# GpSimd's layer-3 bias adds and FFN weight halves moved into layers 1 and 2 of a graph network kernel

## What is computed

```python
xn = _layernorm(x)
# gnn: three layers, widths 256 -> 1024 -> 512 -> 256, each
#   gcn_conv (h = x @ W, summed over edges with coef dinv[src]*dinv[dst]) + b, relu, layer_norm * gamma + beta
x = x + gnn(xn, edges) + mix(xn)
# ffn on xn2 = _layernorm(x): a router picks 1561 of the 3125 nodes...
sel = take_along_axis(xn2, sel_idx)
y = (gelu(sel @ w1 + b1) @ w2 + b2) * w_sel
x = x + (xn2 + scatter(y))
```

## Time and profile before

| what | value |
|---|---|
| median of 3 runs | 1459.4 us (1458.06 to 1460.7) |
| profiled execution, its own time | 1460.05 us |
| its span in the profile | 1458.2 us |
| its mean granted TensorE clock | 0.959 of full speed |
| busy: PE / DVE / ACT / POOL | 1283.3 / 821.0 / 524.8 / 530.6 us |

### The profile page before, as it was taken

One profiled execution on the slowest core, in us unless ns is written; L12 is line 12 of the kernel. 1 busy time (PEld: TensorE's weight loads), 2 busy tenths in 40 slices (PEclk: granted clock), 3 DMA queues, 4 the chain that ended last, 5 costly groups with the idle time before them and its releaser, 6 DMA issues.

```text
span 1458.2 us, 20220 instructions
## 1 busy us (share of the span) xinstructions
PE 1283.3 (88%) x7100; PEld 866.5 (59%) x7100; DVE 821.0 (56%) x1478; ACT 524.8 (36%) x984; POOL 530.6 (36%) x542
## 2 busy tenths in 40 slices
PE   1996776897679999999999999999999999778985
PEld 1763453654446666666665666666666555457775
DVE  6566677868745545454553222222222998878675
ACT  3323626458532222222221232222221212248952
POOL 1003777777767777776000000000004840223000
PEclk9988888998879999999999999999999999989998
DMA  9860000000323232222210422212222444110002
GB/s 270 285 228 1 1 1 1 1 1 1 90 69 82 52 76 50 75 61 65 72 43 24 121 65 65 64 46 62 64 64 66 131 126 129 44 44 1 1 1 88
DMA packets 46192, 99.52 MB, mean 68 GB/s; under 512 B 19079, under 2 KB 31252, under 8 KB 46002
## 3 DMA queue, kind: packets, MB, share of 16 engines
q1 hardware_dynamic: 32814, 98.55, 23.8%
q0 software_dynamic: 13312, 0.13, 0.7%
HBM read 75.79 MB, written 22.85 MB: 68 GB/s over the span
## 4 chain that ended last, share of the span: by engine, by line
PE 66%; DVE 20%; ACT 5%; issue 5%; DMA 1%; POOL 1%; SPq 0%; DVEq 0%; ACTq 0%; POOLq 0%
PE psum L1705 63%; DVE scr L1216 4%; DVE scr L948 3%; PE psum L2066 1%; DVE scr L1174 1%; ACT scr L1367 1%; POOL acc L571 1%; DVE scr L1167 1%; DVE big L1151 1%; DVE scr L1178 1%; DMA rows<-in_x 1%; DVE scr L1164 1%; DVE scr L1161 1%; DVE acc L1233 1%; PE psum L2044 1%
## 5 line engine op out<-in xcount | busy, mean ns | idle before, releaser
L550 POOL DMA_INDIRECT counts<-big,eidx x416 | 422.7, 1016 | 252.7 <-issue 130.9
L1705 PE MATMUL psum<-rows,scr 125*125 125x512 f16 x1250 | 278.3, 381 | 11.5 <-DVE scr L1164 9.3
L1705 PE MATMUL psum<-big,scr 125*125 125x512 f16 x1250 | 278.5, 379 | 1.0 <-DVE big L1068 1.0
L1705 PEld LDWEIGHTS psum<-rows,scr 125*125 125x125 f16 x1250 | 170.4, 137 | 113.3 <-DVE scr L1164 10.0
L1705 PEld LDWEIGHTS psum<-big,scr 125*125 125x125 f16 x1250 | 169.9, 137 | 95.2 <-DVE big L1068 1.5
L566 POOL MEMSET big<- 128x4 f16 x1 | 0.1, 115 | 422.1 <-PE psum L1705 422.1
L1705 PE MATMUL psum<-wb,scr 128*125 128x512 f16 x600 | 137.5, 379 | 1.4 <-DVE scr L1051 1.4
L1032 DVE TENSOR_SCALAR scr<-psum,col 125x256 f32<-125x256 f32 x25 | 12.1, 485 | 172.1 <-PE psum L1705 172.1
L1705 PEld LDWEIGHTS psum<-wb,scr 128*125 128x125 f16 x600 | 81.1, 136 | 45.8 <-DVE scr L1051 1.9
L1705 PE MATMUL psum<-big,wm 128*128 128x313 f32 x312 | 95.0, 455 | 12.3 <-ACT big L1420 7.2
L1705 PE MATMUL psum<-wb,big 128*125 128x256 f16 x600 | 75.7, 280 | 23.8 <-DVE big L1227 21.1
(11 more groups left out here) (367 smaller groups left out, 1909.1 us busy)
## 6 DMA issues: line engine op xcount, KB each, us to landing
scr<-counts SPq DMA_DIRECT2D x75, 683.6 KB
counts<-wb SPq DMA_DIRECT2D x25, 683.6 KB
counts<-big,eidx POOLq DMA_INDIRECT x416
scr<-counts SPq DMA_DIRECT2D x75, 79.3 KB
scr<-in_x SPq DMA_DIRECT2D x25, 125.0 KB
rows<-in_x SPq DMA_DIRECT2D x5, 560.0 KB
out<-acc SPq DMA_DIRECT2D x5, 560.0 KB
wb<-in_w SPq DMA_DIRECT2D x1, 2048.0 KB, 10.6
```

What stands on the lines that cost most here:

```text
L550: pool.indirect_dma_start(cells, bass.IndirectOffsetOnAxis(ap=eidx[:, r * EQ + g:r * EQ + g + 1], axis=0), evalue[:, at_c:at_c + 1], None, ...
L1705: return pe.matmul(o, l, r, start=start, stop=stop)
```

## The change

GpSimd's program is put in another order: the 25 adds of `be3` and the eight weight pieces now stand ahead of the two clears of pad columns. The adds wait for `fx_done` of all 25 tiles, which DVE reaches in the last tile of layer 1, and for rows loaded long before. The pieces wait for `fscale_done`. To give these scales earlier, the PE sums, ACT's root and DVE's seven small instructions move from the front of layer 3 to a point after tile 8 of layer 2. For that, tiles 5 to 8 of layer 2 are written out on PE, DVE and ACT, and their loop runs 4 passes (from 1 to 4) in place of 5. No computation is added or left out.

```diff
 # GpSimd
-        pool.wait_ge(sem("rows1_ready"), T)
-        pool.memset(free(nT16[1], P * G, ...), 0.0).then_inc(sem("npad_done"), 1)
-        pool.wait_ge(sem("lo2_done"), T)
-        pool.wait_ge(sem("agg_done"), 2 * T)
-        pool.memset(free(nT16[0], P * G, ...), 0.0).then_inc(sem("npad_done"), 1)
-
         pool.wait_ge(sem("rowa_loaded"), 16 * 5)
         pool.wait_ge(sem("fx_done"), T)
         for t in range(T):
             pool.tensor_tensor(accv[:, t, :], accv[:, t, :], be3r, ALU.add).then_inc(sem("be3_added"), 1)
         pool.wait_ge(milestone("fscale_done"), AFTER["fscale_done"])
...
+        pool.wait_ge(sem("rows1_ready"), T)
+        pool.memset(free(nT16[1], P * G, ...), 0.0).then_inc(sem("npad_done"), 1)
+        pool.wait_ge(sem("lo2_done"), T)
+        pool.wait_ge(sem("agg_done"), 2 * T)
+        pool.memset(free(nT16[0], P * G, ...), 0.0).then_inc(sem("npad_done"), 1)
 # VectorE, layer 2
-        for t in range(HEAD):
+        for t in range(HEAD + RING):
             step2(t, t % 2, first=t == 0)
-        with dve.Fori(0, LOOPS) as i:
+        dve.wait_ge(milestone("fnorm_done"), AFTER["fnorm_done"])
+        (the seven instructions that end in fscale_done, from ahead of layer 3)
+        with dve.Fori(1, LOOPS) as i:
 # ScalarE, layer 2
         ffn_norms()
-        with act.Fori(0, LOOPS) as i:
+        for t in range(HEAD, HEAD + RING):
+            step2(t, t % 2)
+        ffn_norms_rooted()
+        with act.Fori(1, LOOPS) as i:
...
-        ffn_norms_rooted()
         root3_(0)
 # TensorE, layer 2
-        with pe.Fori(0, LOOPS) as i:
+        for t in range(HEAD, HEAD + RING):
+            step2(t, t, None)
+        pe.wait_ge(sem("fsquares_done"), 1)
+        (the 10 matmuls that end in fsum_done, from ahead of layer 3)
+        with pe.Fori(1, LOOPS) as i:
```

More of the change, by code:

```diff
@@ L561, in _ @@
                            pattern=[[-1, 128]], channel_multiplier=1).then_inc(sem("tri"), 1)
-        pool.wait_ge(sem("rows1_ready"), T)
-        pool.memset(free(nT16[1], P * G, [[CW, 4], [1, 1]]), 0.0).then_inc(sem("npad_done"), 1)
-        pool.wait_ge(sem("lo2_done"), T)
-        pool.wait_ge(sem("agg_done"), 2 * T)
-        pool.memset(free(nT16[0], P * G, [[CW, 4], [1, 1]]), 0.0).then_inc(sem("npad_done"), 1)
         pool.wait_ge(sem("rowa_loaded"), 16 * 5)
@@ L583, in _ @@
             pool.wait_ge(sem("fpiece_done"), c + 1)
+        pool.wait_ge(sem("rows1_ready"), T)
+        pool.memset(free(nT16[1], P * G, [[CW, 4], [1, 1]]), 0.0).then_inc(sem("npad_done"), 1)
+        pool.wait_ge(sem("lo2_done"), T)
+        pool.wait_ge(sem("agg_done"), 2 * T)
+        pool.memset(free(nT16[0], P * G, [[CW, 4], [1, 1]]), 0.0).then_inc(sem("npad_done"), 1)
         def stage_rows(c):
@@ L1124, in step2 @@
                 normalise(t, pre[b][:, 0:D2], D2, "relu2_done", "xhat2_done")
-        for t in range(HEAD):
+        for t in range(HEAD + RING):
             step2(t, t % 2, first=t == 0)
-        with dve.Fori(0, LOOPS) as i:
+        dve.wait_ge(milestone("fnorm_done"), AFTER["fnorm_done"])
+        done.did(dve.tensor_scalar(f_back, fnorm[:, 0:2], 1e-20, 1.0 / F16_TOP, ALU.max, ALU.mult))
+        done.did(dve.tensor_scalar(g_back, fnorm[:, 0:1], float(D) ** 0.5, fnorm[:, 2:3], ALU.mult, ALU.add))
+        done.settle()
+        done.did(dve.tensor_scalar(g_back, g_back, 1e-20, 1.0 / F16_TOP, ALU.max, ALU.mult))
+        done.did(dve.tensor_scalar(hid_back, f_back[:, 0:1], 1.0 / NORMED, None, ALU.mult))
+        done.settle()
+        done.did(dve.reciprocal(g_scale, g_back))
+        done.did(dve.tensor_tensor(out_back, g_back, f_back[:, 1:2], ALU.mult))
+        dve.reciprocal(f_scale, f_back).then_inc(milestone("fscale_done"), 1)
+        with dve.Fori(1, LOOPS) as i:
             done.enter(i, 3 * 4)
+            done.base = i * (3 * 4) + (done.outer - 3 * 4)
             for k in range(HEAD, HEAD + RING):
                 step2(i * RING + k, k % 2)
-            done.leave(LOOPS)
+            done.leave(LOOPS - 1)
         step2(T, T % 2, last=True)
@@ L1181, in step3 @@
             row_stats(summed, st4, mv4, 4)
[L1184 to L1193, removed]
         STEP3 = 10
@@ L2130, in _ @@
             step2(t, t, None, first=t == 0)
-        with pe.Fori(0, LOOPS) as i:
+        for t in range(HEAD, HEAD + RING):
+            step2(t, t, None)
+        pe.wait_ge(sem("fsquares_done"), 1)
+        for n, columns in enumerate(((0, 1), (2, 3), (4,))):
+            for k in columns:
+                last = mm(bank(6, 128, 1, n), ones[:, :], ssf[:, k:k + 1], k == columns[0], k == columns[-1])
+        last.then_inc(sem("fsum_done"), 1)
+        with pe.Fori(1, LOOPS) as i:
             for k in range(HEAD, HEAD + RING):
@@ L2153, in step3 @@
             aggregate(2, t, k, k % 2, both, loads(2, k, i), "pre3_done", free_from(t, k, i), previous)
[L2156 to L2160, removed]
         pe.wait_ge(sem("lo3_done"), T - 2)
```

## The result

The changed kernel takes 1453.6 us in the median of 15 runs, the kernel before 1460.7 us in 15 runs beside them; the ratio is 0.9959, with a 95% interval from 0.9946 to 0.9971. The ratio is taken between the means of the runs, which is why it gives a little less than the two medians do. It is a gain of 6.0 us, between 4.2 and 7.9. The forecast was 7.4 us.

The account below looks back on a forecast made before the run. The prediction took DVE's backlog in layer 3, started late by GpSimd's adds, as the bound. Its terms, -6.4 - 1.3 + 0 + 0.3 = -7.4 us, gave 1452.0 us; own range 1451 to 1453.5, 8 in 10 from 1449.5 to 1456.0.

Parts of the forecast that it names:

- The adds leave the front of layer 3: At layer 3's start, DVE begins tile 0 when PE has finished it, 6.4 us earlier (bounds 6.0 and 6.7).
- The pieces leave tiles 0 to 4: In layer 3, tiles 0 to 4 run at PE's pace, 27.0 us in place of 28.29, gaining 1.3 us.
- From tile 5 on only the origin moves: In layer 3, DVE's old timetable from tile 5 to tile 21 stays, moved earlier by 7.7 us.
- four tiles written out: In layer 2, the same instructions in a straight line cost PE 0; DVE's 0.33 us loop turn is off the path.
- PE's ten sums, 1.17 - 1.17 = 0: Moved from layer 3's front to behind tile 8 of layer 2; PE is busy in both places, so cost 0.
- DVE waits for the root in layer 2, cost 0: After tile 8, 4.4 us of cover for the root and seven DVE instructions; without it 1.4 us once.
- The adds beside the end of layer 1, cost 0: GpSimd's adds run beside layer 1's end, where DVE has 6.4 us of cover; cost 0, upper bound 0.7.
- The pieces beside layer 2, 0.3 us: In layer 2, GpSimd's pieces may hold L1114, whose cover is 1.40 us; 0.3 us cost, bounds 0 and 3.4.
- Rival A: Contention only moves and part lands on PE in layers 1 and 2, giving back 2 to 4.1 us; chance 0.14.
- Rival B: No gain shows: stage_rows and PE alone pace layer 3, longer stops use up the earlier start; 1457 to 1460; chance 0.06.
- Rival C: Slower: pieces hold DVE's normalise chain in layer 2 until PE stands still, up to 1481 us; chance 0.03.
- Rival D: More gain: stage_rows falls partly into DVE's idle moments in layer 3, sparing PE a stop; 1447.7 us; chance 0.05.

Follow-up runs that it names:

- Run 1: Against the kernel before, only the be3 adds move ahead of the pad clears; scales and weight pieces stay at layer 3's front; ratio 0.9940.
- run 8: Against the kernel before: be3 adds moved ahead, stage_rows instructions cut in fifths, its third pass held until behind the router; ratio 0.9836.
- run 3: Against the changed kernel, layer 3 starts in the other PSUM bank, so its first aggregate skips the wait for layer 2's last read-out; ratio 0.9968 to the kernel before.
- run 9: Against the changed kernel, PE makes the ten sums once more ahead of layer 3; span 1450.77 us on the common clock.
- run 4: Against the changed kernel, the third stage_rows waits for xn2 of all 25 tiles; ratio 0.9937 to the kernel before.
- run 5: Against the changed kernel, each of stage_rows' four GpSimd instructions is cut in five, one per tile; ratio 0.9855 to the kernel before.
- run 10: Against the changed kernel, PE makes the ten sums once more behind tile 8 of layer 2; span 1453.38 us on the common clock.
- run 2: Against the changed kernel, the be3 adds go back behind the second pad clear; scales and pieces stay in layer 2; ratio 0.9992 to the kernel before.
- run 6: Against the changed kernel, the third stage_rows waits for all xn2 and two small DVE instructions behind the router; ratio 0.9923 to the kernel before.

## Why the prediction was right, and where its sum was too large

The forecast of 1452.0 us (faster, 7.4 us) met 1453.6 us, 6.0 us faster. That is inside the range for 8 in 10, and 0.1 us outside the forecast's own range of 1451 to 1453.5. The kernel before measured 1.3 us more in these runs than the 1459.4 on which the forecast was built; the ratio applied to 1459.4 gives 1453.4. Its reading of the bound was right: DVE's backlog and not GpSimd's busy share. By steps:

*The adds leave the front of layer 3:* foreseen 6.4 us at tile 0. Run 1 has 6.34, where nothing else is changed. In the full change it is 5.38, and the difference of 1.0 belongs to PE's ten sums, below.

*The pieces leave tiles 0 to 4:* foreseen 27.0 us for five tiles in place of 28.29; measured 1151.36 - 1124.37 = 26.99.

*From tile 5 on only the origin moves:* nearly. The lead of 6.68 us at tile 5 is 6.08 at tile 12 and 5.54 at tile 21, while run 1 keeps 6.05 and 6.03 from tile 5 to 12. Run 1 has DVE's program as it was. In the others DVE idles some 0.42 us at each turn of layer 3's loop in place of 0.33, and in the midst of the loop's body, where it idled nothing, 0.39 us the first time and 0.16 later, on no semaphore. The forecast's "four tiles written out" was costed for layer 2, where nothing was lost; the price came one loop later, about 0.6 us up to tile 12 and another 0.5 to tile 21. It is a term that the sum left out, and it weighs as much as the next one. That it comes from the place of the loop in DVE's program is an inference: the kernels with four tiles written out show it and runs 1 and 8 don't, but these also have the pieces in another place, and no run moved the loop alone.

*PE's ten sums, 1.17 - 1.17 = 0:* this is the step that failed. PE was busy in both places, as the forecast said, but that didn't make the two costs equal. In layer 2 they cost 1.04 us, in front of layer 3 nothing (runs 1, 3 and 9), because PE had to wait for `pre2_done` of the last tile there. The wait was in the code and DVE's L1122 in the trace, but PE showed no idle time for it before, since the sums filled it. The term should have been +1.0: -6.4 - 1.3 + 1.0 = -6.7, which is the 6.68 us of tile 5.

*DVE waits for the root in layer 2, cost 0:* right. Its seven instructions end 7.4 us before PE has anything for it.

*The adds beside the end of layer 1, cost 0:* right; PE's two waits there are 1.4 and 1.0 us in both kernels. *The pieces beside layer 2, 0.3 us:* it was 0. L1114 was held for 0.02 us at most and its cover of 1.40 us was not touched. That a GpSimd instruction can hold L1114 was the premise, and at 937.98 it took 0.55 us inside one of 1.56 us; why it took 0.92 us beside the adds and 0.55 beside this piece stays open. Rival A, and with it the reading at its hardest of the Trainium skill's rule (page "SBUF — State Buffer", section "Who interferes with whom"), didn't come true here, although L1185's 3.15 us beside `stage_rows`' 3.67 us in layer 3 agree with the rule.

Rival B failed at tile 12, where 6.08 us are kept. Rival C is excluded by the ratio's interval. Rival D failed as foreseen: `stage_rows` met DVE in the same phase (7.63 and 8.32 us for tiles 5 and 6, against 7.63 and 8.31).

The sum by what was measured: 5.38 at tile 0, 1.30 on tiles 0 to 4, less 0.60 to tile 12, less 0.54 to tile 21, less 0.12 to tile 24, and 0.43 from the last stretch, 5.85 us. The forecast lost 1.0 us by the sums and 1.3 us between tiles 5 and 24, and was given back 0.3 us that layer 2 did not cost and 0.4 us of the last stretch, which is luck: executions differ by more there.

## What to carry to other kernels

Work that is moved out of a place where its engine seems busy may have been covering a wait: before it is costed at nothing, look for the semaphore that the next instruction waits on and when it would have come. Where GpSimd and VectorE work side by side, cut GpSimd's instructions short before moving them; here that was worth more than twice the change itself, with GpSimd's busy time higher. And compare traces from a row ahead of the change, since executions differed by up to 5 us there and by 2 to 3 us in a race near the end.

## What the runs showed of the hardware

A VectorE instruction on 125x25 numbers took 2.76 us beside a GpSimd instruction of 3.67 us that had begun first (run 4), and 0.24 us without it (the changed kernel). The same GpSimd work in 256-wide instructions of 0.87 us held VectorE's L1189 for 0.1 to 0.4 us (run 5). Not all VectorE instructions were held: the read-outs of PSUM L1172 and L1175 took 0.48 us beside `stage_rows` as without it, and L1114 0.55 us inside a GpSimd instruction of 1.56 us (the changed kernel).

2.15 us of one-column matmuls in the midst of a fully busy TensorE were followed by 1.69 us lost to the lower clock (run 10, one execution); 1.18 us of them (the changed kernel) were not. In runs 1, 2 and 4 the same price, 45.07 us for 200 matmuls in place of 43.38, stood behind PE's stop ahead of tile 14 (1.96, 2.84 and 2.83 us), and tile 21 came 0.9 us later for it. The stop alone doesn't decide it: the changed kernel and runs 3, 6, 9 and 10 had a stop of 2.83 or 2.84 us in the same place and took 43.38 us. From run 1, us and busy us, granted clock 0.83:

```profile
1198.00:1208.00 10.00, 8.69 (x33) 5.17 (x34) 8.52 (x31) 2.79 (x10) 0.00 (x0) 0.83 0.34 85
```
